# Three small reorderings in the head of a category-conditioned residual layer: who asks for the second x tile, when the second weights are asked for, and one-hot before diagonals

## What is computed

```python
def reference(x, itok_B_0_30, L0_cond_W, L0_cond_b):
    # x (128, 128, 512), ids (128,), W (32, 512, 512), b (32, 512)
    selected_W = W[ids]
    selected_b = b[ids]
    return x + einsum('bti,bio->bto', x, selected_W) + selected_b[:, None, :]
```

## Time and profile before

| | |
|---|---|
| time, median of 3 runs | 359.47 us (359.25 to 359.9) |
| the profiled execution's own time | 361.66 us |
| its span in the trace | 360.4 us |
| TensorE busy | 355.8 us (99%), 1553 matmuls |
| GpSimd, VectorE, ScalarE busy | 74%, 48%, 41% |
| DMA | 109.51 MB, mean 304 GB/s |

### The profile page before, as it was taken

One profiled execution on the slowest core, in us unless ns is written; L12 is line 12 of the kernel. 1 busy time (PEld: TensorE's weight loads), 2 busy tenths in 40 slices (PEclk: granted clock), 3 DMA queues, 4 the chain that ended last, 5 costly groups with the idle time before them and its releaser, 6 DMA issues.

```text
span 360.4 us, 6783 instructions
## 1 busy us (share of the span) xinstructions
PE 355.8 (99%) x1553; PEld 290.6 (81%) x1553; DVE 173.7 (48%) x282; ACT 146.5 (41%) x262; POOL 266.7 (74%) x144
## 2 busy tenths in 40 slices
PE   8999999999999999999999999999999999999996
PEld 3788888888888888888888888888888888888885
DVE  6754454455454445444545445445444544544542
ACT  4563253334344344343534334434434334433420
POOL 1777999999549598799973999799979899935000
PEclk9999999999999999999999999999999999999999
DMA  6999998899896988789997799999997999965622
GB/s 225 333 360 355 378 367 320 299 360 378 304 297 233 384 299 306 273 294 368 357 339 268 268 384 328 305 313 367 328 334 269 361 369 315 325 198 195 193 103 103
DMA packets 43381, 109.51 MB, mean 304 GB/s; under 512 B 4817, under 2 KB 4818, under 8 KB 38610
## 3 DMA queue, kind: packets, MB, share of 16 engines
q1 hardware_dynamic: 37730, 70.01, 54.6%
q0 software_dynamic: 5328, 38.28, 31.0%
q10 hardware_dynamic: 288, 0.79, 0.7%
HBM read 75.50 MB, written 33.55 MB: 303 GB/s over the span
## 4 chain that ended last, share of the span: by engine, by line
PE 97%; DMA 1%; DVE 0%; SPq 0%; issue 0%
PE pA L447 96%; DMA xs<-xt 1%; PE pA L459 1%; PE pA L470 1%; DMA idr<-ids 0%; DVE os L398 0%; DVE top L342 0%; DVE key L339 0%; SPq L179 0%; SPq L180 0%; SPq L162 0%; DVE best L339 0%
## 5 line engine op out<-in xcount | busy, mean ns | idle before, releaser
L398 DVE TENSOR_TENSOR os<-pA,bb 128x512 f32<-128x512 f32 x128 | 88.5, 691 | 170.4 <-PE pA L447 169.9
L305 ACT ACTIVATE xh<-xs 128x512 fp32r<-128x512 f32 x127 | 80.3, 633 | 196.2 <-PE pA L447 123.2
L274 POOL TENSOR_TENSOR wl<-wr,wh 128x2048 fp32r<-128x2048 f32 x30 | 138.7, 4622 | 2.5
L447 PE MATMUL pA<-wh,xh 128*128 x508 | 135.8, 389 | 0.0
L447 PE MATMUL pA<-wl,xh 128*128 x508 | 135.8, 389 | 0.0
L447 PE MATMUL pA<-wh,xl 128*128 x508 | 135.6, 389 | 0.0
L447 PEld LDWEIGHTS pA<-wh,xh 128*128 128x128 f32 x508 | 95.3, 188 | 20.1 <-issue 0.2
L447 PEld LDWEIGHTS pA<-wh,xl 128*128 128x128 f32 x508 | 95.3, 188 | 19.8
L447 PEld LDWEIGHTS pA<-wl,xh 128*128 128x128 f32 x508 | 95.3, 188 | 19.8
L363 DVE TENSOR_TENSOR xl<-pT,xh 128x512 fp32r<-128x512 f32 x127 | 86.6, 682 | 10.6 <-ACT pT L308 10.5
L270 POOL TENSOR_SCALAR wh<-wr 128x2048 fp32r<-128x2048 f32 x30 | 57.5, 1918 | 37.3 <-PE pA L447 35.5
(11 more groups left out here) (48 smaller groups left out, 20.5 us busy)
## 6 DMA issues: line engine op xcount, KB each, us to landing
xs<-xt SPq DMA_DIRECT2D x128, 256.0 KB, 5.4
out<-os SPq DMA_DIRECT2D x128, 256.0 KB, 5.1
wr<-w POOLq DMA_DIRECT2D x29, 1024.0 KB, 7.6
bb<-bias POOLq DMA_DIRECT2D x7, 1024.0 KB, 9.3
wr<-w SPq DMA_DIRECT2D x2, 512.0 KB, 6.2
wr<-w SPq DMA_DIRECT2D x1, 1024.0 KB, 6.2
wr<-w ACTq DMA_DIRECT2D x1, 512.0 KB, 3.9
bb<-bias SPq DMA_DIRECT2D x2, 256.0 KB, 7.0
```

Of the source, the lines that this page charges most:

```text
L274: eng.tensor_tensor(wl[:, at], wr[:, c % NR, :], wh[:, at].bitcast(f32), ALU.subtract).then_inc(s_wp if c == 2 else s_w, 1)
L305: eng.activation(xh[:, i % NH, :, :], xs[:, i % NX, :, :], ACT.Copy).then_inc(s_xh, 1)
L398: eng.tensor_tensor(os[:, i % NO, :], pA[i % NA][:, :], bb[:, bass.ds(at, D)], ALU.add)._wait_ge(s_mm, i + 2).then_inc(s_fin, 1)
L447: mm = eng.matmul(pA[i % NA][:, :], xp[:, i % NH, k, :], wp[:, bass.ds(at + k * D, D)], start=(n == 0), stop=(n == 3 * KT - 1))
```

## The change

Four edits, all in the head:

- ScalarE, after its small first activation, waits for `top`, reads the second key and asks for tile 1 on its own DMA queue. SP no longer does.
- SP asks for the first half of category 1's weights right after the last piece of category 0's, ahead of its wait for `top` and its read of the eight keys.
- VectorE makes the one-hot matrices right after the rank, and adds the first diagonal after them.
- TensorE runs 3 narrow warm matmuls fewer ahead of the table matmul and 3 more after it.

```diff
--- before.py
+++ after.py
@@ -179,6 +179,7 @@
             eng.load(lead, best[:, :].bitcast(i32))
             x_load(eng, 0, bass.ds(eng.snap(lead, min_val=BITS, max_val=BITS + (C + 1) * B - 1) % B, 1))
             eng.dma_start(raw(0, 3, KT), W[0, :, 3 * D:]).then_inc(s_w0[2], 16)
+            w1_load(0)
             eng.wait_ge(s_t0, 2)
             eng.load(first, top[0:1, :])
             ahead = table(eng, "la", tbc, B, 0, B - 1)
@@ -193,8 +194,6 @@
                     eng.wait_ge(s_pt, i - NX)
                 x_load(eng, i, bass.ds(b, 1))
 
-            load(1)
-            w1_load(0)
             load(2)
             load(3)
             bias_load(eng, 0, 1, s_b0[0])
@@ -287,6 +286,10 @@
             eng.dma_start(raw(0, 2, 3), W[0, :, 2 * D:3 * D]).then_inc(s_w0[1], 16)
             eng.wait_ge(s_one, 1)
             eng.activation(spare[:, :], ones[:, 0:1], ACT.Copy)
+            second = eng.alloc_register("second")
+            eng.wait_ge(s_t0, 2)
+            eng.load(second, top[0:1, 1:2])
+            x_load(eng, 1, bass.ds(eng.snap(second, min_val=EXP, max_val=EXP + (C + 1) * B - 1) % B, 1))
 
             def high_0(ks, done):
                 eng.wait_ge(s_x[0], 16)
@@ -348,11 +351,11 @@
             link(eng.scalar_tensor_tensor(out=cmp[:, :], in0=pS[:, 0:128], scalar=colf[:, 0:1], in1=dif[:, :],
                                           op0=ALU.subtract, op1=ALU.is_lt))
             link(eng.reduce_sum(rank[:, :], cmp[:, :], AX.X))
-            eng.wait_ge(s_cst, 2)
-            add_one(0)
             eng.tensor_scalar(hot[:, 0:B], iot[:, :], rank[:, 0:1], None, ALU.is_equal).then_inc(s_hot, 1)
             eng.tensor_scalar(num[:, 1:2], colf[:, :], 1.0 / B, None, ALU.mult).then_inc(s_hot, 1)
             eng.tensor_scalar(hot[:, B:], thr[:, :], colf[:, 0:1], None, ALU.is_gt).then_inc(s_hot, 1)
+            eng.wait_ge(s_cst, 2)
+            add_one(0)
             add_one(1)
             eng.wait_ge(s_bat, 1)
             eng.tensor_scalar(tbc[:, :], pS[0:3, 0:B], num[0:3, 0:1], None, ALU.add).then_inc(s_tab, 1)
@@ -412,14 +415,13 @@
             eng.matmul(pS[:, 128:129], idb[:, :], unit[:, 0:1], start=True, stop=True)
             eng.matmul(pS[:, 0:128], unit[:, :], idb[:, :], start=True, stop=True).then_inc(s_col, 1)
             warm(4)
-            warm(3, 128)
             lowest = eng.alloc_register("lowest")
             eng.wait_ge(s_t0, 2)
             eng.load(lowest, top[0:1, 0:1])
             eng.wait_ge(s_one, 3)
             eng.wait_ge(s_hot, 3)
             eng.matmul(pS[0:3, 0:B + C], num[:, :], hot[:, :], start=True, stop=True).then_inc(s_bat, 1)
-            warm(3, 128)
+            warm(6, 128)
 
             HH, HL, LH = 0, 1, 2
             first = [(p, k) for p in (HH, HL, LH) for k in HIGH]
```

## The result

| | before | after |
|---|---|---|
| median, first comparison (11 and 11 runs) | 359.90 us (359.25 to 360.36) | 361.62 us (360.41 to 363.75) |
| ratio, 95% interval | | 1.0048 (1.0029 to 1.0066) |
| median, second comparison (35 and 12 runs) | 359.82 us | 360.65 us (359.95 to 361.51) |
| ratio, 95% interval | | 1.0020 (1.0007 to 1.0033) |
| profiled execution, its span | 361.66, 360.4 us | 360.60, 359.3 us |

The change makes the kernel slower, by 0.2 to 0.5%. But the changed kernel's trace is the shorter one of the two. Both facts have to be explained: the runs of the changed kernel spread over 3.3 us, those of the one before over 1.1 us, and the profiled execution before was none of the usual ones.

The account below looks back on a forecast made before the run. It took TensorE's `batch` matmuls as the bound, with only the head before 12 us open to change. Terms +0.15 (tile 0) + 0 + 0 + 0 on 359.47 gave 359.6 us, range 358.6 to 361.0.

Parts of the forecast that it names:

- What bounds the kernel now: Whole kernel: `batch` matmuls fill TensorE from about 12 us, 345 us; only the head before 12 us can give time.
- The second x tile: Head, ScalarE requesting tile 1 at about 3.6 us: no gain, tile 0 lands later, +0.15 us at the end.
- the delay d: Tile 0's later landing beside tile 1's traffic: taken as 0.3 us, range -0.3 to +0.7.
- Costs only d/2: TensorE's head at half clock until about 10.2 us: a start slipping by d costs half of it, +0.15 us.
- The gain is nothing in this trace: Tile 1 landing perhaps 1.1 us earlier gives 0: ScalarE did not wait for it, TensorE takes it only at 11.95.
- Rival 1: Head without the profile: the second tile binds, so an earlier one gives up to 1.1 us, 358.4 us; chance 0.17.
- The weights' first half: SP's request at about 4.0 instead of 5.12 us: cannot overtake tile 0, GpSimd gains 0.5 us at most; worth nothing.
- One-hot ahead of diagonals: VectorE in the head: first diagonal at most +0.07 us later, hidden; table matmul to about 5.2 us; gain 0.
- the warm matmuls: TensorE before tile 0: three narrow ones moved, idle time grows from 0.77 to about 1.3 us; sum 0.
- Rival 2: TensorE's head: more idle time before tile 0 makes the clock rise later, costing 1.5 us, 361.1 us; chance 0.20.
- The rule of the Trainium skill on turns between queues: DMA engines alternate between queues by packets: tile 0's share would go out ahead of tile 1's, sum 0; not used.

Follow-up runs that it names:

- the last experiment: Kernel before, SP reading the second key alone and requesting tile 1 right behind block 3: 0.9994 twice; with one-hot and warm matmuls moved too, 359.39 us, 0.9984.
- both loads: Kernel before with ScalarE's request of tile 1 and the weights' half ahead of SP's key reads; one-hot and warm matmuls as before: 360.20 us, ratio 1.0018.
- the repeat of ScalarE's request: Kernel before with only ScalarE's request of tile 1, run again on one chip with its twin with more warm matmuls: 360.11 us, ratio 1.0030.
- the run that held ScalarE's request: Changed kernel, with ScalarE's request of tile 1 put behind the first half of tile 0's high part: 365.33 us in 5 runs, ratio 1.0156.

## Why the prediction was wrong

Forecast: 359.6 us, 358.6 to 361.0, within 0.2% with 0.60. Measured: 361.62, ratio 1.0048. The second comparison's 360.65 lies inside the range, but is slower by more than the noise too (1.0020, from 1.0007). The traces account for 0.8 to 1.0 us, by a late tile 0 and a late block 3; the rest of the first comparison's 1.7 us comes with its 5 long runs in 11. Step by step:

- **"What bounds the kernel now"**: `batch` as the bound from 12 us on, and the head as the only place for a difference, held in every trace. The head itself was read from one execution, which was rare in two ways: tile 0 took 4.14 us (2.7 to 2.9 in nine other traces without a neighbour) and the clock rose after 10 us. The prediction saw the sign of it, 2.2 us between that execution and the median, put it down to the profiling and used it for one rival only. Profiling doesn't do that: the second profiled execution of before took 359.60 us.
- **"The second x tile": the delay d.** This term was mis-sized. Taken: landing at 7.22 plus 0.3. Measured with a neighbour on the second queue: 2.7 to 4.9 us in ten traces, 3.9 in both of the changed kernel, against 2.8: d = 1.1 us, outside the bound of 0.7. The bound divided 256 KB by the 358 GB/s of a full stretch; the engines were busy and moved 218, and at that rate 256 KB take 1.2 us. "Costs only d/2" failed with the late clock that it leaned on.
- **"The gain is nothing in this trace"**: true of that trace alone. Where the clock is up early, TensorE waited for tile 1 (1.22 us in one trace). Rival 1 was right that this can happen; that the last experiment gains by it is not shown. This change could not collect it, since block 3's copy stands ahead of tile 1's high part.
- **The term that is missing** is block 3. The prediction followed what queues behind on SP and never asked what tile 1's traffic does to block 3, requested 0.2 us after it: 5.5 and 5.4 us to land in place of 3.6, and TensorE, ScalarE and with it tile 1's high part wait for it. In the changed kernel's traces `batch` starts 0.8 to 1.0 us later for it (10.79 and 10.67 against 9.84), and block 3 is what ends last. A third to a half of that the late tile 0 would have cost alone: with tile 0 at 6.8 and 6.9 us and block 3 at 8.3 and 8.5, early enough that TensorE doesn't wait for it, `batch` starts at 10.13 and 10.24 (both loads; the repeat of ScalarE's request).
- **"The weights' first half"** was right in part: it does not delay tile 0 (2.7 and 2.9 us with it and without a neighbour), and block 3 by little (3.5 us in the run that held ScalarE's request, 4.2 in the run of the half alone, 3.6 without). With tile 1 behind it on SP's queue it does harm, 5 of 12 long runs; the change avoids that.
- **"One-hot ahead of diagonals"** and **"the warm matmuls"**: costed at nothing, measured at 1.0001 (0.9980 to 1.0021). Right as far as that interval tells; the table matmul came at 5.21, forecast 5.2.
- **Rival 2** named the right kind of loss and its price, 1.5 us: from the first product to `batch` the three traces with a fallen clock behind a late tile 0 take 4.83 to 4.85 us, against 3.3 at full clock. But it put it on the wrong cause, and left out the late tile 0 that comes with it. It is not that the rise comes later since the warm matmuls were moved (alone they made no long run in 12). In every trace but the first one the clock is up for the first tile's split products or earlier, and in these it falls once a late tile 0 has left TensorE idle: 0.50 behind 8 us, 1.00 again from 11.5 in the trace of ScalarE's request alone. Of the 5 long runs of the first comparison 3 are of this kind by their mean granted clock (0.995); what the other 2 are (363.48 and 363.75 us, 1.00) no trace shows. The Trainium skill (TensorE: Matmul & The Clock Gate, Part 1) has the clock follow activity. The traces agree that it falls behind idle time, from 1.00 in the stretch up to 8 us to 0.50 after it. But the idle time alone does not settle it: with 1.21 us of it the clock fell in one trace, and with 1.22, 1.24 and 1.31 us (one-hot reordering alone, tile 1 ahead of block 3, the changed kernel again) it stayed at 1.00.
- **The rule of the Trainium skill on turns between queues** (DMA: Bandwidth & Descriptors, Queues, rings and completion order) would have had tile 0 go out ahead of tile 1, at no cost. The traces speak against that use of it: tile 0 took 3.8 us with tile 1 requested 0.3 us behind it on the other queue, 2.8 without (2.7 to 4.9 in all traces of the one kind, 2.7 to 2.9 in all but one of the other). Its other statement, that requests of several engines run on the same 16 DMA engines, is what every trace here shows.

## What to carry to other kernels

Ask for the first data that the critical engine needs, and let nothing stand beside it on another queue; a request that is "free" on an idle engine's queue is paid in the landing of its neighbours, here typically 1.1 us for the tile before it and up to 1.9 us for the piece after it. Before resting a sum on one profiled execution of a short head, compare its time with the median: 2 us apart meant another execution than the usual one. And where TensorE is kept warm for data, warm work that ends before a late landing leaves the idle time there, and work that goes on past an early one delays the real matmuls; both were seen here, and a gain by the longer warm work was not shown.

## What the hardware showed that was not expected

- A DMA request in ScalarE's list does not wait for the activations ahead of it: at 3.66 us it went out 0.07 us after the start of an activation of 0.61 us that stands ahead of it in the list.
- The same 256 KB take from 2.7 to 4.9 us to land with nearly the same request time. What else is in flight accounts for part of that; the same kernel has 2.8 and 4.1 us in two traces, and another 3.8 and 4.9.
- The clock fell when TensorE had already started its real work, not during the idle time: 1.00 from 6.1 to 8.0 us with 1.68 us idle, 0.50 from 9 to 10.
- Executions of over 363 us exist in which the granted clock never fell on record; they are half of the long runs with a neighbour, and 6 of 8 of the kernel before.
